# The first pair's group norm, split and crossbar transfers, moved between the low-rank merges of the weight preparation

## The reference

```python
def _gn(v, G=32, eps=1e-5):            # 32 groups of 24 channels, over all tokens of an image
    g = v.reshape(B_, H_, W_, G, C_ // G)
    m = jnp.mean(g, axis=(1, 2, 4), keepdims=True)
    s = jnp.var(g, axis=(1, 2, 4), keepdims=True)
    return ((g - m) / jnp.sqrt(s + eps)).reshape(v.shape)

qkv = x @ qkv_w.T + qkv_b              # qkv_w: 2304 x 768
qkv[..., :768]  += x @ la_q.T @ lb_q.T # low rank, 4
qkv[..., 1536:] += x @ la_v.T @ lb_v.T
attn = softmax((q * scale) @ k.T + rel_h + rel_w)   # 12 heads of 64, biases from q and rel_pos
out  = x + (attn @ v) @ proj_w.T + proj_b
```

## Time and profile before

| | |
|---|---|
| median of three runs | 3306.41 us (3306.01 to 3306.46) |
| profiled execution | 3306.87 us |
| its span, first to last instruction | 3304.9 us |
| busy in the span | PE 97%, DVE 83%, ACT 64%, POOL 1% |
| mean granted TensorE clock | 0.99 of full speed |
| DMA | 420.09 MB, mean 127 GB/s |
| ScalarE's only table load | 1283 ns, at 51.14 us |

### The profile page before, as it was taken

How to read it: one execution, slowest core, us unless ns; L and a number is a source line. 1 busy time by engine, 2 the same in 40 slices (tenths; PEclk the granted TensorE clock), 3 DMA queues, 4 the chain that set the end, 5 groups by cost and what they waited for, 6 DMA issues and landing times.

```text
span 3304.9 us, 78573 instructions
## 1 busy us (share of the span) xinstructions
PE 3199.2 (97%) x31280; PEld 1996.5 (60%) x31280; DVE 2751.1 (83%) x5490; ACT 2125.2 (64%) x5491; POOL 35.2 (1%) x65
## 2 busy tenths in 40 slices
PE   7499999999999999999999999999999999999999
PEld 4255666666666666666666666666666666666665
DVE  7688888888888888888888888888888888888875
ACT  2366666666666666666666666666666666666664
POOL 0100000000000000000000000000000000000000
PEclk9799999999999999999999999999999999999999
DMA  3157765667776666766666776566776666776656
GB/s 130 39 104 140 141 124 117 123 129 143 142 130 122 118 133 136 144 137 119 119 129 129 149 137 123 118 122 133 143 141 127 123 122 132 138 142 133 119 107 127
DMA packets 1265503, 420.09 MB, mean 127 GB/s; under 512 B 1092754, under 2 KB 1245026, under 8 KB 1265138
## 3 DMA queue, kind: packets, MB, share of 16 engines
q1 hardware_dynamic: 1248898, 376.49, 59.6%
q10 hardware_dynamic: 16240, 38.58, 3.9%
HBM read 86.60 MB, written 38.54 MB: 38 GB/s over the span
## 4 chain that ended last, share of the span: by engine, by line
PE 65%; DVE 22%; ACT 7%; issue 3%; DMA 1%; SPq 0%; POOL 0%; POOLq 0%
PE ring L633 34%; PE ring L700 13%; PE score L676 6%; DVE split L901 5%; ACT prob L786 5%; PE o_ps L690 5%; DVE sums L927 3%; DVE row_max L879 3%; PE ring L655 3%; PE ring L724 2%; DVE split L893 1%; DVE x_sb L951 1%; DVE rel_sb L872 1%; DVE k_lo L846 1%; DVE sums L932 1%
## 5 line engine op out<-in xcount | busy, mean ns | idle before, releaser
L633 PE MATMUL ring<-xn,w_hi 128*128 128x392 f16 x6912 | 1712.2, 328 | 12.1 <-DMA xn<-xs 12.0
L633 PE MATMUL ring<-xn,w_lo 128*128 128x392 f16 x3456 | 1133.1, 328 | 0.0
L786 ACT ACTIVATE prob<-score,neg_max,exp_scale 98x196 f32<-98x196 f32 x1536 | 769.8, 510 | 305.6 <-DVE neg_max L883 302.0
L633 PEld LDWEIGHTS ring<-xn,w_hi 128*128 128x128 f16 x6912 | 642.9, 96 | 481.0 <-DMA xn<-xs 11.9
L901 DVE SCALAR_TENSOR_TENSOR split<-prob,row_inv,split 98x196 f16<-98x196 f32 x1536 | 545.6, 418 | 9.0
L879 DVE TENSOR_REDUCE row_max<-score 98x4 f32<-98x784 f32 x384 | 372.2, 969 | 168.6 <-PE score L676 168.5
L633 PEld LDWEIGHTS ring<-xn,w_lo 128*128 128x128 f16 x3456 | 331.6, 96 | 244.0 <-issue 2.6
L700 PE MATMUL ring<-o_hi,w_hi 128*128 128x392 f16 x1116 | 368.0, 330 | 0.0
L700 PE MATMUL ring<-o_hi,w_lo 128*128 128x392 f16 x1116 | 367.1, 329 | 0.0
L700 PE MATMUL ring<-o_lo,w_hi 128*128 128x392 f16 x1116 | 367.1, 329 | 0.0
L796 ACT ACTIVATE split<-prob,row_inv 98x196 f16<-98x196 f32 x768 | 310.4, 454 | 72.5 <-DVE row_inv L887 71.7
(11 more groups left out here) (134 smaller groups left out, 4531.7 us busy)
## 6 DMA issues: line engine op xcount, KB each, us to landing
x_sb<-in_x ACTq DMA_DIRECT2D x32, 1176.0 KB
y_sb<-in_x SPq DMA_DIRECT2D x186, 196.0 KB
out<-y_sb SPq DMA_DIRECT2D x186, 196.0 KB
rel_q<-rel_sb SPq DMA_DIRECT2D x128, 122.5 KB, 2.3
stage<-in_L_conv_qkv_w SPq DMA_DIRECT2D x3, 2304.0 KB, 14.8
turned<-split SPq DMA_TRANSPOSE x384, 4.2
rel_q<-rel_sb SPq DMA_DIRECT2D x128, 24.5 KB, 2.2
v_tok<-v_split SPq DMA_TRANSPOSE x192, 3.7
```

The source lines that it names most:

```text
L633: last = T.matmul(ring[:, bank, 0:NT], w[:, c, 128 * j:128 * j + 128], xn[:, par, xx, :, c, 0:HALF], start=(c == 0 and part == 0), stop=(c ...
L786: last = A.activation(prob[:, head, half, :], score[0:HALF, head, TOK * half:TOK * half + TOK], ACT.Exp, bias=neg_max[:, k % 2, i:i + 1], ...
```

## The change

In `prepare`:

- The load of x of pair 0 is issued in front of the four weights.
- The buffers and semaphores of the norm now live in `build`, so that both blocks have them. la lies inside the still unused half of xn.
- VectorE's and TensorE's streams hold pair 0's norm between the merges and the low-rank tiles. ScalarE squares and rounds, GpSimd makes the power, and SP issues the four crossbar transfers.
- GpSimd zeroes mx, then makes minus_half, ones and the zeroes of xs, before onehot and mask; VectorE waits for `consts_made` just in front of the maximum of k_w and for the mask (`masks_made`) only where it is used.

In `attend`, `sequence` leaves out the norm's kinds for pair 0, so the ring of banks doesn't hold its three G steps either.

```diff
+NORM = ("A", "B", "U", "D", "G", "E", "H", "I", "L", "XT")
 def sequence(order, pairs, last=()):
     return [(kind, q - old, k) for q in range(-2, pairs) for kind, old, k in (order if q < pairs - 1 else last)
-            if 0 <= q - old < pairs]
+            if (1 if kind in NORM else 0) <= q - old < pairs]
...
 # prepare, SP
+            sp.dma_start(x_sb[:, :, :], g["x_rows"][0]).then_inc(g["x_in"], 16)
             for i, src in ((0, g["qkv_w"][0:C]), (1, g["qkv_w"][C:2 * C]), (2, g["qkv_w"][2 * C:3 * C]),
                            (3, g["proj_w"])):
...
-            sp.dma_start(g["x_sb"][:, :, :], g["x_rows"][0]).then_inc(g["x_in"], 16)
+            for part, made in enumerate((xs_hi_made, xs_lo_made)):
+                for image in range(2):
+                    sp.wait_ge(made, image + 1)
+                    sp.dma_start_transpose(xn[:, 0, part, 2 * image:2 * image + 2].rearrange("p b c r -> p (b c) r"),
...
 # prepare, ScalarE
+            act.wait_ge(xs_zeroed, 1)
+            for image, two in enumerate(halves):
+                act.wait_ge(centred, image + 1)
+                A.activation(squares[:, two], x_sb[:, two, :], ACT.Square).then_inc(squared, 1)
+            for image, two in enumerate(halves):
+                act.wait_ge(normed, image + 1)
+                A.activation(xs[0:HALF, 0, two], x_sb[:, two, :], ACT.Copy).then_inc(xs_hi_made, 1)
 # prepare, GpSimd, behind the constants
+            pool.wait_ge(read_G, 2)
+            G.tensor_tensor(inv_dev[:, :], var_eps[:, :], minus_half[:, :], ALU.pow).then_inc(inv_dev_made, 1)
             pool.wait_ge(maxima, 1)
 # prepare, VectorE: merge(n) is the old body of the loop over the low-rank tiles
-            dve.wait_ge(consts_made, 1)
...
+            dve.wait_ge(g["x_in"], 16)
+            for image in range(2):
+                V.tensor_reduce(sums[:, image, :], by_group(image), AX.XY, ALU.add).then_inc(summed, 1)
+            merge(0)
+            dve.wait_ge(done_G, 1)
+            V.tensor_copy(mean[:, :, :] ...
+            merge(1)
+            dve.wait_ge(read_G, 1)
+            ... two subtractions of the mean, then_inc(centred, 1) each
+            merge(2)
+            ... two sums of squares, each behind dve.wait_ge(squared, image + 1)
+            merge(3)
+            dve.wait_ge(done_G, 2)
+            V.tensor_scalar(var_eps[:, :], ring[0:2 * GROUPS, 1, 0:1], EPS, None, ALU.add).then_inc(read_G, 1)
+            merge(4)
+            dve.wait_ge(inv_dev_made, 1)
+            V.tensor_scalar(diagonal[:, :], ...
+            merge(5)
+            dve.wait_ge(done_G, 3)
+            V.tensor_copy(rstd[:, :, :] ...
+            dve.wait_ge(consts_made, 1)
+            dve.wait_ge(w_in[1], 16)
+            maximum(1)
+            ... two multiplications by rstd, then_inc(normed, 1) each
+            merge(6)
+            ... two subtractions for the low part, each behind dve.wait_ge(xs_hi_made, image + 1)
+            for n in range(7, 2 * CT):
+                merge(n)
             dve.wait_ge(w_in[3], 16)
             maximum(3)
 # prepare, TensorE: lora(n) is the old body of its loop
+            lora(0)
+            pe.wait_ge(summed, 2)
+            T.matmul(ring[0:HALF, 0, 0:2 * GROUPS], gmean[:, :], both, start=True, stop=True).then_inc(done_G, 1)
+            for n in range(1, 4):
+                lora(n)
+            pe.wait_ge(summed, 4)
+            T.matmul(ring[0:2 * GROUPS, 1, 0:1], both, gmean[:, 0:1], start=True, stop=True).then_inc(done_G, 1)
+            for n in range(4, 6):
+                lora(n)
+            pe.wait_ge(diagonal_made, 1)
+            T.matmul(ring[0:HALF, 2, 0:2 * GROUPS], ones[:, :], diagonal[:, :], start=True, stop=True).then_inc(done_G, 1)
+            for n in range(6, 2 * CT):
+                lora(n)
```

More of the change, by code:

```diff
@@ L243, in build @@
         x_sb = sb(keep, "x_sb", [HALF, 4, C], F32)
-        x_in = keep.enter_context(nc.semaphore("x_in"))
+        xs = sb(keep, "xs", [128, 2, 4, C], F16)
+        xn = sb(keep, "xn", [128, 2, 2, 4, CT, ROWS], F16)
+        squares = xs[0:HALF].rearrange("p a b c -> p (a b c)").bitcast(F32).rearrange("p (b c) -> p b c", b=4)
+        sums = sb(keep, "sums", [HALF, 2, GROUPS], F32)
+        mean = sb(keep, "mean", [HALF, 2, GROUPS], F32)
+        rstd = sb(keep, "rstd", [HALF, 2, GROUPS], F32)
+        var_eps = sb(keep, "var_eps", [2 * GROUPS, 1], F32)
+        inv_dev = sb(keep, "inv_dev", [2 * GROUPS, 1], F32)
+        minus_half = sb(keep, "minus_half", [2 * GROUPS, 1], F32)
+        diagonal = sb(keep, "diagonal", [2 * GROUPS, 2 * GROUPS], F32)
+        ones = sb(keep, "ones", [2 * GROUPS, HALF], F32)
+        keep_sem = lambda name: keep.enter_context(nc.semaphore(name))
+        x_in, xn_in = keep_sem("x_in"), keep_sem("xn_in")
+        summed, centred, squared = keep_sem("summed"), keep_sem("centred"), keep_sem("squared")
+        inv_dev_made, diagonal_made = keep_sem("inv_dev_made"), keep_sem("diagonal_made")
+        normed, xs_hi_made, xs_lo_made = keep_sem("normed"), keep_sem("xs_hi_made"), keep_sem("xs_lo_made")
+        done_G, read_G = keep_sem("done_G"), keep_sem("read_G")
         x_rows = x.rearrange("(n b) h w c -> (n b h w) c", b=2).rearrange("(n t p) c -> n p t c", t=4, p=HALF)
@@ L256, in prepare @@
     ident, gmean, bias, pw, inv = g["ident"], g["gmean"], g["bias"], g["pw"], g["inv"]
+    x_sb, xs, xn, squares = g["x_sb"], g["xs"], g["xn"], g["squares"]
+    sums, mean, rstd, ones = g["sums"], g["mean"], g["rstd"], g["ones"]
+    var_eps, inv_dev, minus_half, diagonal = g["var_eps"], g["inv_dev"], g["minus_half"], g["diagonal"]
+    summed, centred, squared, normed = g["summed"], g["centred"], g["squared"], g["normed"]
+    inv_dev_made, diagonal_made, xn_in = g["inv_dev_made"], g["diagonal_made"], g["xn_in"]
+    xs_hi_made, xs_lo_made, done_G, read_G = g["xs_hi_made"], g["xs_lo_made"], g["done_G"], g["read_G"]
+    halves = (slice(0, 2), slice(2, 4))
     NR = 2 * H - 1
@@ L385, in _, with merge @@
                                   ).then_inc(lbT_made, 1)
[L387 to L390, removed]
+            def merge(n):
+                j = lora_tiles[n]
                 dve.wait_ge(w_in[j // CT], 16)
@@ new lines, in _ @@
+            merge(0)
+            dve.wait_ge(done_G, 1)
+            V.tensor_copy(mean[:, :, :].rearrange("p n g -> p (n g)"), ring[0:HALF, 0, 0:2 * GROUPS]).then_inc(read_G, 1)
+            merge(1)
+            dve.wait_ge(read_G, 1)
+            for image, two in enumerate(halves):
+                rows = x_sb[:, two, :].rearrange("p b (g c) -> p b g c", c=GP)
+                V.tensor_tensor(rows, rows, spread(mean, image), ALU.subtract).then_inc(centred, 1)
+            merge(2)
+            for image, two in enumerate(halves):
+                dve.wait_ge(squared, image + 1)
+                V.tensor_reduce(sums[:, image, :], squares[:, two].rearrange("p b (g c) -> p g b c", c=GP),
+                                AX.XY, ALU.add).then_inc(summed, 1)
@@ new lines, in _ @@
+            dve.wait_ge(consts_made, 1)
+            dve.wait_ge(w_in[1], 16)
+            maximum(1)
+            dve.wait_ge(read_G, 3)
+            for image, two in enumerate(halves):
+                rows = x_sb[:, two, :].rearrange("p b (g c) -> p b g c", c=GP)
+                V.tensor_tensor(rows, rows, spread(rstd, image), ALU.mult).then_inc(normed, 1)
+            merge(6)
+            for image, two in enumerate(halves):
+                dve.wait_ge(xs_hi_made, image + 1)
+                V.tensor_tensor(xs[0:HALF, 1, two], x_sb[:, two, :], xs[0:HALF, 0, two],
+                                ALU.subtract).then_inc(xs_lo_made, 1)
@@ L491, in attend @@
     x_sb, x_in, x_rows = g["x_sb"], g["x_in"], g["x_rows"]
+    xs, xn, squares = g["xs"], g["xn"], g["squares"]
+    sums, mean, rstd, ones = g["sums"], g["mean"], g["rstd"], g["ones"]
+    var_eps, inv_dev, minus_half, diagonal = g["var_eps"], g["inv_dev"], g["minus_half"], g["diagonal"]
+    summed, centred, squared, normed = g["summed"], g["centred"], g["squared"], g["normed"]
+    inv_dev_made, diagonal_made = g["inv_dev_made"], g["diagonal_made"]
+    xs_hi_made, xs_lo_made, xn_in = g["xs_hi_made"], g["xs_lo_made"], g["xn_in"]
     out_rows = g["out"].rearrange("(n b) h w c -> (n b h w) c", b=2).rearrange("(n t p) c -> n p t c", t=4, p=HALF)
@@ L522, in attend @@
         row_inv = S("row_inv", [HALF, 2, 4], F32)
[L523 to L530, removed]
         ring = own.enter_context(nc.psum_tensor("ring", [128, BANKS, 512], F32))
```

49 lines of the change are left out of this document (28 added, 21 removed).

## The result

The changed kernel takes 3288.28 us (median of five runs, 3286.59 to 3289.20) against 3306.46 us before (3306.01 to 3306.74): ratio 0.9943, 95% interval 0.9932 to 0.9954. The profiled execution took 3287.48 us, its span 3285.6; before 3306.87 and 3304.9. So 19.4 us less in the profiled execution and 18.2 in the medians, where I had 20.1. A second set of five gave 3288.29 us, ratio 0.9943 (0.9930 to 0.9955). Between sets the median of the kernel before lay anywhere from 3306.17 to 3307.35 us, so a difference between medians of two sets is good to about 1 us.

A forecast was written before the change was run, and what follows sets the result against it. TensorE, busy 97% of the span, bounds the kernel, so only its idle start could be saved: -31.3 + 11.2 = -20.1 us, giving 3286.8 from the profiled execution or 3286.3 from the median; forecast 3286.5 us, range 3282.5 to 3291.5.

The forecast's parts named there:

- Out of the start of the attention: Start of the attention: pair 0's norm of 31.6 us falls away except about 0.3 us, -31.3 us.
- lbT without the constants: Preparation: lbT's copies no longer wait for GpSimd's constants and start at 7.7 instead of 10.41, -2.7 us.
- Added to DVE: Preparation: pair 0's norm adds ten large and four small operations to VectorE's stream, 17.6 us.
- x and q_w: Preparation loads: x there near 8.9 to 9.5, each weight 2.9 us later; only q_w late, by 1.0 us.
- Rival D: Preparation loads: the weights are later than 2.9 us, or x is; 3289 to 3291 us, chance 0.06.
- The waits between the merges: VectorE's preparation: 1.5 us at merge 4; tiles 9 to 11 come 0.3, 0.7 and 0.7 us late.
- The low-rank tiles at 2.56 us: TensorE's preparation: tiles cost 2.56 us everywhere, as the stage already runs at the lower clock and can't lose.
- The power: GpSimd's preparation: the 7.7 us run while GpSimd waits, so the power near 30 pays nothing, nor does pair 1's.
- Rival B: GpSimd's power: the code load is exposed behind the wait, +3.3 us, up to +5.4; 3290 and 3295, chance 0.07.
- The slow start of the first Q tile: First projection: the clock still falls, so the first Q tile keeps its 5.71 us instead of 3.0.
- All behind it shifts: Behind the first projection: everything hangs on it and both kernels keep the same order, so all of it shifts.
- rival E: Steady pairs: moved bank positions and new addresses slow them; at 0.8 us more per pair 3311 us, chance 0.03.

The follow-up runs named there:

- mx_only: Kernel before, with VectorE waiting for the constants in front of the maximum of k_w and no longer in front of lbT: 3303.49 us against 3306.17, ratio 0.9992.
- x_first: Kernel before, with the load of x issued ahead of the four weights and the norm left in place: 3307.03 us against 3306.17, ratio 1.0002.
- second profile of the changed kernel: The changed kernel itself run once more, with no edit: 3288.29 us.
- pow_twice: Kernel before, with one more power (64 values, result unused) on GpSimd ahead of the all-reduce: 3306.58 us against 3307.35, ratio 0.9998.
- pow_first: Kernel before, with GpSimd's memsets of v_split and split moved behind the first power: 3306.44 us against 3306.17, ratio 1.0000.

## Why the prediction was right, point by point

The sum and its mechanism held: the norm's chain left the start of the attention, and the preparation grew by what I had walked through, within 1 us. One term was mis-sized, the load of x.

- *Out of the start of the attention, -31.3 us.* Right: DVE's last copy of the preparation ends at 99.85, TensorE starts at 100.15, and nothing waits for the crossbar transfers.
- *lbT without the constants, -2.7.* Right: -3.1 here (7.35), and mx_only shows it alone, -2.8.
- *Added to DVE, 17.6 us.* Right: the ten large ones last as before, beside merges or not.
- *x and q_w.* The mis-sized term. x came at 11.3 (said: 8.9 to 9.5), q_w was used at 16.77 (said: 14.9). DVE waited 1.13 + 2.04 = 3.2 us, against 1.0. I took x's share of the bytes, 2.9 us; q_w came 4.0 us later in x_first (16.0 for 12.0), 3.9 in the second profile of the changed kernel (15.93) and 4.8 in the first, with 268 GB/s where the weights have over 400. Why two executions of one kernel differ by 0.8 us is open. Low-rank tile 1 was ready by then, so 0.65 us of a wait that I had counted vanished, lbT was 0.3 us early, and of the 1.9 us 0.9 were left at the end: the last small operation ended at 70.9 instead of 70.0 (at 70.0 in the second profile). Rival D had its direction.
- *The waits between the merges.* Said 1.5 at merge 4, 0.5 at 5 and 0.3, 0.7, 0.7 at the end; measured 1.48, 0.46, 0.25, 0.62, 0.62.
- *The low-rank tiles at 2.56 us.* Right behind gaps of TensorE of up to 5.84 us; the reading of the weight loads held. The granted clock column reads 1.00 in this stage of the kernel before and 0.50 from 12 us on in the changed kernel, and the tiles take 2.56 us in both: the stage had no clock to lose.
- *The power.* Rival B is out, by the change's own trace. I had the gap hidden behind GpSimd's idle time; pow_twice shows that ahead of the all-reduce there was none to hide, since a power with no idle time before it started at once, at 10.28. Behind the all-reduce the hiding is as I argued: pair 1's power started 0.1 us after its operand (153.87 + 0.14, then 154.11), with 48.74 us of idle time before it.
- *The slow start of the first Q tile.* It was at 0.50 up to 103 us, 4.55 us long where I had kept 5.71. In the second profile it is 5.25, and over all kernels that don't keep TensorE busy 4.55 to 6.05: how soon the clock rises differs from execution to execution, so the 1.2 us won against my 5.71 are luck.
- *All behind it shifts.* Right to 1 us: up to the power of pair 1 the gain shrank from 19.3 to 18.2 (x of pair 1 took 7.12 instead of 6.43 us, the two Q tiles 7.67 instead of 5.99, against 1.2 won on the first), and over the pairs it came back. That return of 1.1 us is within what these pairs differ by from kernel to kernel (next point), so it asks for no cause. Why the medians gained 18.2 and 18.7 us and not my 20.1 is open beyond the 0.9 us of the preparation.
- *Pairs unchanged (rival E).* Powers of pairs 1 to 31 take 2943.2 us before and 2942.1 after, 2941.2 to 2944.1 in all other kernels. By my own test, pairs 2 to 31, it is 2850.2 and 2849.3, with 2848.4 to 2850.9 in the others: not the same to the digit, as I had asked, but 1 us lower and within the spread. The moved banks and addresses cost nothing to be seen.

The balance of the profiled execution: -31.3 + 12.1 (70.87 against 58.75) = -19.2, with 0.1 us of small differences behind it -19.3 at the first projection, and -19.4 at the end.

## What to carry to other kernels

Much of a serial prologue is waiting, here 14.0 of the 31.6 us for VectorE. Cut into pieces between the work of another stage, it is not free but costs what it adds to the engine that sets that stage's pace: 12.1 us in place of 31.3 (17.6 us of VectorE's work, less 3.1 of an earlier start and the idle time that it fills). But price the piece that its data come in: a load's place in the queue costs its time at its own rate, not its bytes at the queue's. Look at which work an idle GpSimd does beside DVE before placing memsets: one that moves into the path can hold a small DVE instruction for its whole length. And behind a removed stall, look at what the next one hangs on: here a load that could be issued 50 us earlier, and a clock that fell in pauses, were worth another 11 us together with VectorE's relief, which is about half of it.

## What the runs showed of the hardware that was not expected

- Two memsets on GpSimd, one behind the other, held a tensor_scalar of DVE for 5.0 us (5.23 instead of 0.25 us, pow_first). Sums beside a memset were not held, nor was a subtraction (92.30, 3.43 us for two, beside the memset of v_split, in the kernel before).
- GpSimd's first power behind the all-reduce started 6.9 to 7.7 us after its work before, in all six kernels with the norm in the old place. An all-reduce behind a power started at once, but it always had 16 us or more of idle time ahead of it.
- While x (98 partitions) was loaded beside weights, the DMA rate fell to 235 to 287 GB/s with the engines fully busy (share 1.02 to 1.06 in stretches of 2 us), against 409 to 418 for the weights alone (128 partitions, share 1.03). Loaded alone, from 29 to 32 us in the kernel before, x had 295 to 323 GB/s at a share of 0.88 to 0.91. The runs don't tell why.
- The low-rank tiles took 2.56 us whether the granted clock column read 1.00 (before) or 0.50 (after).
